# The last five items of a query convolution taken group by group, and an attention core's transposes split around values and projection

## The reference

```python
qkv = x @ w_qkv.T
q = _causal_conv1d(_causal_conv1d(q, qc1_w, qc1_b, N_HEADS), qc2_w, qc2_b, 1)   # 1024 channels, 3 taps
k = _causal_conv1d(_causal_conv1d(k, kc1_w, kc1_b, N_KV), kc2_w, kc2_b, 1)      # 256 channels
q = q.reshape(B, S, 16, 64) + 0.5 * k_mean[:, :, None, :]
k = k.reshape(B, S, 4, 64) + 0.5 * q_mean[:, :, None, :]
q, k = _rope(_l2norm(q), cos, sin), _rope(_l2norm(k) * key_temp, cos, sin)
scores = jnp.where(causal, jnp.einsum('bhqd,bhkd->bhqk', q, kg) * scale, min)
out = jnp.einsum('bhqk,bhkd->bhqd', softmax(scores), vg)
return out @ w_o.T
```

## Time and profile before

| | us |
|---|---|
| median of three runs | 2670.66 |
| the profiled execution | 2671.36 |
| its span in the trace | 2669.6 |
| query convolution, from the start of item 27 to the last matmul | 384.4 to 426.3 |
| from there to the first transpose of the attention core | 426.3 to 444.9 |
| attention core's units, first scores to last projection | 460.5 to 688.1 |

### The profile page before, as it was taken

The page is one execution under the profiler, slowest core; times in us unless marked ns, Lnnn a source line. Parts: engine busy times, 40 slices in busy tenths (PEclk is TensorE's granted clock), DMA queues, the critical chain, the costliest instruction groups (busy, mean ns, idle before and its releaser), DMA issues. The chain is left out here.

```text
span 2669.6 us, 37362 instructions
## 1 busy us (share of the span) xinstructions
PE 2489.1 (93%) x12664; PEld 1816.4 (68%) x12664; DVE 1777.2 (67%) x3189; ACT 1419.6 (53%) x2796; POOL 1490.2 (56%) x1274
## 2 busy tenths in 40 slices
PE   7999996799899789999999999999999999999967
PEld 3464443444587668878878878887787787787754
DVE  2044456577423687777777777778778778778765
ACT  2210003555222286686676676776776776776713
POOL 0043354455101248678678678677777768668642
PEclk9999998899899899999999999999999999999979
DMA  4012321000210263253352352352352352343300
GB/s 163 0 38 75 118 59 36 1 1 1 87 63 13 69 187 108 88 159 100 95 157 94 100 156 91 97 166 89 98 167 87 100 163 91 100 150 101 104 19 32
DMA packets 143628, 241.87 MB, mean 91 GB/s; under 512 B 28368, under 2 KB 48592, under 8 KB 143184
## 3 DMA queue, kind: packets, MB, share of 16 engines
q1 hardware_dynamic: 143440, 239.48, 28.7%
HBM read 232.08 MB, written 7.34 MB: 90 GB/s over the span
## 5 line engine op out<-in xcount | busy, mean ns | idle before, releaser
L1785 ACT ACTIVATE mix<-mix,sc 128x128 f32<-128x128 f32 x1024 | 310.8, 389 | 3.0 <-DMA sc<-head_scal 2.8
L2116 POOL TENSOR_TENSOR xend<-xdt,sc 128x384 f32<-128x384 f32 x128 | 106.7, 834 | 320.0 <-DVE xdt L1918 320.0
L1955 DVE SCALAR_TENSOR_TENSOR feat<-ps,chan,feat 128x511 f32<-128x511 f32 (+2 forms) x384 | 283.8, 739 | 1.8
L98 PE MATMUL ps<-xt_hi,w_in_hi 128*128 128x512 f32 x640 | 267.3, 418 | 12.8 <-ACT sg L1775 5.7
L1944 DVE TENSOR_TENSOR mix<-mix,cb 128x512 f32<-128x512 f32 x256 | 272.2, 1068 | 1.2 <-ACT mix L1791 1.2
L99 PE MATMUL ps<-xt_lo,w_in_hi 128*128 128x512 f32 x640 | 253.6, 396 | 0.0
L100 PE MATMUL ps<-xt_hi,w_in_lo 128*128 128x512 f32 x640 | 253.6, 396 | 0.0
L2132 POOL TENSOR_TENSOR w_in_lo<-w_in_raw,w_in_hi 128x512 fp32r<-128x512 f32 x158 | 211.6, 1339 | 61.1 <-ACT w_in_hi L1740 61.1
L1989 DVE TENSOR_TENSOR y_lo<-y,y_hi 128x512 fp32r<-128x512 f32 x128 | 183.0, 1430 | 81.1 <-ACT y_hi L1801 81.0
L1632 PE MATMUL ps<-w_o_hi,y_hi 128*128 128x512 f32 x512 | 207.6, 405 | 7.9 <-DVE y_lo L1989 4.3
L98 PE MATMUL ps<-xt_hi,w_g_hi 128*128 128x512 f32 x512 | 212.8, 416 | 2.2 <-DVE feat L1955 2.2
(11 more groups left out here) (288 smaller groups left out, 5943.9 us busy)
## 6 DMA issues: line engine op xcount, KB each, us to landing
mix<-row_cum SPq DMA_DIRECT2D x128, 512.0 KB, 5.7
w_in_raw<-in_w_conv_in SPq DMA_DIRECT2D x160, 256.0 KB, 3.1
w_g_raw<-in_w_gate_in SPq DMA_DIRECT2D x128, 256.0 KB, 3.5
ecb<-row_ecum SPq DMA_DIRECT2D x256, 96.0 KB, 3.4
w_o_raw<-in_w_out SPq DMA_DIRECT2D x64, 256.0 KB, 3.0
w<-in_w_c2q SPq DMA_DIRECT2D x16, 768.0 KB, 5.3
w<-in_w_c2q SPq DMA_DIRECT2D x16, 512.0 KB, 3.7
wqkv<-in_w_qkv SPq DMA_DIRECT2D x1, 3072.0 KB, 14.0
```

The costliest lines, as they stand in the source:

```text
L98: pe.matmul(out, a_hi, b_hi, start=(n == 0), stop=False)
L1785: last = act.activation(m, m, ACT.Relu, bias=sc[:, b, CUM, z, 2 * i + e:2 * i + e + 1], scale=-1.0)
L1955: dve.scalar_tensor_tensor(out=to, in0=ps[:, j % 2, 0:S - back], scalar=chan[:, bb % B, j, K1 - 1 - back:K1 - back], in1=to, op0=ALU.mult, ...
```

## The change

In the convolution `TAIL` becomes 5, with `EXTRA` = 2 items (30 and 31) that own buffers outside the rings: the space of `k1` for their token differences, of `w2k` and `head_sum` for their taps. These were last read by the key convolution, so that SP, DVE and POOL wait for `c2_ready` at `NK` there. Nothing in `schedule` moves.

```diff
-    NI, RAWK = 4 * QT, 4
+    NI, RAWK, EXTRA = 4 * QT, 4, 2
-            TAIL = WS
+            TAIL = WS + EXTRA
+            def tx_of(r, kind):
+                if last(r) < 0:
+                    return tx[:, r % WS, kind, :, :]
+                flat = k1[:, :, :, :].rearrange("p c b n -> p (c b n)")
...
+            def outer_taps(r):
+                if last(r) < 0:
+                    return w2[:, r % RAWS, 0:TAPS:2, :]
+                if last(r) == 0:
+                    return w2k[:, :, :, :].rearrange("p c t o -> p (c t o)")[:, 0:2 * BANK].rearrange("p (t o) -> p t o", t=2)
+                return head_sum[:, 0, :, :]
...
+            def freed(eng, r):
+                if last(r) >= 0:
+                    eng.wait_ge(c2_ready, NK)
+                elif r >= WS:
+                    eng.wait_ge(item_done, r - WS + 1)
...
                     for r in range(RAWS, NI):
                         p, n, c = pass_of(r)
-                        if inner_item(r - RAWS):
+                        if last(r) >= 0:
+                            sp.wait_ge(c2_ready, NK)
+                        elif inner_item(r - RAWS):
```

```diff
                         if u < NU:
                             scores(u)
+                        if 1 <= u < NU + 1:
+                            turn(u - 1, (0, 1))
                         if u % 2 == 1 and 3 <= u < NU + 3:
                             values((u - 3) // 2)
                         if u >= KV0 + LAG:
                             project(u - KV0 - LAG)
                         if 1 <= u < NU + 1:
-                            turn(u - 1)
+                            turn(u - 1, (2, 3))
...
                             for i in range(GQ):
+                                if i == GQ - 1:
+                                    copy(u - 1, 0)
...
-                        if u >= 1:
-                            for k in range(units[u - 1][1] + 1):
...
+                        for k in range(1 if u < NU else 0, ZB):
+                            copy(u - 1, k)
```

More of the change, by code:

```diff
@@ L246, in attention @@
             w1_loaded = core.sem("a_w1_loaded")
-            w2_loaded = [core.sem(f"a_w2_loaded{i}") for i in range(RAWS)]
+            w2_loaded = [core.sem(f"a_w2_loaded{i}") for i in range(RAWS + EXTRA)]
             small_loaded = core.sem("a_small_loaded")
@@ L451, in attention, with last, loaded @@
             ROPE_AT = 2 * QT + 2
-            TAIL = WS
+            TAIL = WS + EXTRA
+            def last(r):
+                return r - (NI - EXTRA)
+            def tx_of(r, kind):
+                if last(r) < 0:
+                    return tx[:, r % WS, kind, :, :]
+                flat = k1[:, :, :, :].rearrange("p c b n -> p (c b n)")
+                at = (2 * last(r) + kind) * B * PAIRS
+                return flat[:, at:at + B * PAIRS].rearrange("p (b n) -> p b n", b=B)
+            def outer_taps(r):
[4 more added lines that the diff above has]
+                return head_sum[:, 0, :, :]
+            def loaded(eng, r):
+                if last(r) < 0:
+                    eng.wait_ge(w2_loaded[r % RAWS], 16 * (r // RAWS + 1))
+                else:
+                    eng.wait_ge(w2_loaded[RAWS + last(r)], 16)
+            def freed(eng, r):
[3 more added lines that the diff above has]
+                    eng.wait_ge(item_done, r - WS + 1)
             def schedule(prepare, rope_k, evict, rope_q):
@@ L493, in _ @@
                         else:
-                            sp.dma_start(w2[:, r % RAWS, 0:TAPS:2, :], taps[:, 0:TAPS:2, :]).then_inc(w2_loaded[r % RAWS], 16)
+                            sp.dma_start(outer_taps(r), taps[:, 0:TAPS:2, :]).then_inc(
+                                w2_loaded[r % RAWS if last(r) < 0 else RAWS + last(r)], 16)
                 @blk.tensor
@@ L515, in item @@
                         if closing:
-                            pe.wait_ge(w2_loaded[r % RAWS], 16 * (r // RAWS + 1))
+                            loaded(pe, r)
                         else:
@@ L527, in item @@
                             for kind in range(2):
-                                taps = w2[:, r % RAWS, 2 * kind, :] if closing else mixed[:, r % WS, kind, :]
-                                last = pe.matmul(ps[:, 2 * j + kind, :], tx[:, r % WS, kind, b, half * P:(half + 1) * P], taps,
+                                taps = outer_taps(r)[:, kind, :] if closing else mixed[:, r % WS, kind, :]
+                                done = pe.matmul(ps[:, 2 * j + kind, :], tx_of(r, kind)[:, b, half * P:(half + 1) * P], taps,
                                                  start=(c == 0), stop=(c == QT - 1 and not closing))
                             if j == JT - 1:
-                                last.then_inc(item_done, 1)
+                                done.then_inc(item_done, 1)
                             elif c == QT - 1 and not closing:
-                                last.then_inc(pass_ready, 1)
+                                done.then_inc(pass_ready, 1)
                             if c == QT - 1 and closing:
@@ L537, in item @@
                                     tokens = head_sum[:, 1, b, half * 2 * P + e:(half + 1) * 2 * P:2]
-                                    last = pe.matmul(ps[:, 2 * j + e, :], tokens, sel[:, 0:BANK], start=False, stop=True)
-                                last.then_inc(pass_ready, 1)
+                                    done = pe.matmul(ps[:, 2 * j + e, :], tokens, sel[:, 0:BANK], start=False, stop=True)
+                                done.then_inc(pass_ready, 1)
                     for r in range(NI - TAIL):
@@ L551, in prepare @@
                         even, odd = q1[:, c, :, 0, :], q1[:, c, :, 1, :]
-                        if r >= WS:
-                            dve.wait_ge(item_done, r - WS + 1)
+                        freed(dve, r)
                         if inner_item(r):
-                            dve.tensor_tensor(tx[:, r % WS, 0, :, :], odd[:, :, 0:PAIRS], even[:, :, 1:], ALU.add).then_inc(t_one, 1)
+                            dve.tensor_tensor(tx_of(r, 0), odd[:, :, 0:PAIRS], even[:, :, 1:], ALU.add).then_inc(t_one, 1)
                             dve.wait_ge(ends_done, inner_before(r + 1))
@@ L560, in prepare @@
                         else:
-                            dve.tensor_tensor(tx[:, r % WS, 0, :, :], even[:, :, 0:PAIRS], even[:, :, 1:], ALU.subtract).then_inc(t_one, 1)
+                            dve.tensor_tensor(tx_of(r, 0), even[:, :, 0:PAIRS], even[:, :, 1:], ALU.subtract).then_inc(t_one, 1)
                     def evict(p, j):
@@ L689, in prepare @@
                             pool.tensor_tensor(ends[:, r % 2, :], w2[:, r % RAWS, 0, :], w2[:, r % RAWS, 2, :], ALU.add).then_inc(ends_done, 1)
-                        if r >= WS:
-                            pool.wait_ge(item_done, r - WS + 1)
+                        freed(pool, r)
                         if inner_item(r):
-                            pool.tensor_tensor(tx[:, r % WS, 1, :, :], even[:, :, 1:], odd[:, :, 0:PAIRS], ALU.subtract).then_inc(t_two, 1)
+                            pool.tensor_tensor(tx_of(r, 1), even[:, :, 1:], odd[:, :, 0:PAIRS], ALU.subtract).then_inc(t_two, 1)
                         else:
-                            pool.tensor_tensor(tx[:, r % WS, 1, :, :], odd[:, :, 1:], odd[:, :, 0:PAIRS], ALU.subtract).then_inc(t_two, 1)
+                            pool.tensor_tensor(tx_of(r, 1), odd[:, :, 1:], odd[:, :, 0:PAIRS], ALU.subtract).then_inc(t_two, 1)
                     def rope(u):
@@ L805, in scores, with turn @@
                                       kt[at, kv, b * S:b * S + wide], start=True, stop=True).then_inc(sc_ready, 1)
-                    def turn(u):
+                    def turn(u, tiles):
                         b, z, kv = units[u]
-                        for k in range(z + 1):
+                        for k in tiles:
+                            if k > z:
+                                continue
                             n = tiles_before[u] + k
@@ L867, in _, with copy @@
                             act.activation(dst, ps[:, n % 4, :].rearrange("p (i n) -> p i n", i=4), ACT.Copy).then_inc(turn_done, 1)
+                    def copy(u, k):
+                        if u < 0 or k > units[u][1]:
+                            return
+                        n = tiles_before[u] + k
+                        act.wait_ge(pt_ready, n + 1)
+                        if u >= 4:
+                            act.wait_ge(pv_ready, (u - 4) // 2 + 1)
+                        act.activation(prob_t[:, u % 4, k, :, :],
+                                       ps[:, 4 + n % 2, :].rearrange("p (i n) -> p i n", i=GQ), ACT.Copy).then_inc(pt_done, 1)
                     for u in range(NU + 1):
```

## The result

The changed kernel takes 2658.42 us (median of five runs, 2656.71 to 2660.05) against 2671.05 us for the kernel before, measured again beside it. The ratio is 0.9952, 95% interval 0.9937 to 0.9966. The forecast was 2660, with 0.80 for faster.

The account below looks back on a forecast made before the run. The normalising and rotating chain was taken to bound the convolution's tail, with 20.8 us of PE copy waits in the core. Tail -4.9, core -4.3 and clock -1.6 sum to -10.8 us, forecasting 2660 us, range 2650 to 2667.

Parts of the forecast that it names:

- The tail: End of the query convolution: group 0 starts two items earlier, PE becomes the limit, the block ends 4.9 us earlier.
- The core, orders and waits: Attention core: PE's split and ACT's earlier copy of tile 0, walked through 32 iterations, save 4.3 us.
- The offsets from D: Attention core, times after DVE's first mask addition: copy 0 at 3.67 us, fourth exponent at 4.2, copy 1 at 4.86.
- +0.9: Attention core, up to iteration 17: time given back after the first batch's gain of 3.9 us, leaving 2.9.
- the late exponent: Attention core: the fourth exponent comes 0.2 us later behind the early copy, delaying the last inversion where DVE limits.
- The clock: Core's first batch: shorter waits ahead of tile 2 remove one of three falls to half clock, saving 1.6 us.
- 3.9 + 1.6: Core's first batch: 3.9 us gained by the walk through the iterations, plus 1.6 us for one clock fall gone.
- A: Rival: the walk holds with no change in the clock, -9.2 us, 2661.5 us; chance 0.54 counted together with the forecast.
- C: Rival: only the tail gains, the core's gain lost as PE waits for normalised probabilities; 2665.8 us, chance 0.12.
- D: Rival: the core gains but the tail doesn't, taps or POOL's difference being late by 4 us or more; 2665, chance 0.09.
- B: Rival: the clock stays up in the core's whole first batch, 5.5 us more gain, 2654 us; chance 0.19.
- E: Rival, slower: ACT's copy 0 holds the fourth exponent for its whole 0.6 us in every unit; 2685 us, chance 0.06.

Follow-up runs that it names:

- e1: Changed kernel with the attention core's order as before, so only the convolution's tail changed: 2661.33 us, ratio 0.9965 to the kernel before.
- e3: Changed kernel with item 31's preparation moved ahead of rope_q(6) in the common order of DVE, ACT and POOL: 2656.06 us.
- e8: Changed kernel with ACT's early copy only for units of three or four key tiles, the old order for narrower ones: 2655.95 us.
- e5: Changed kernel with ACT's order as before, all copies behind the four exponents; PE's split stays: 2662.70 us.
- e6: Changed kernel with PE's order as before, the whole turn behind values and projection; ACT's early copy stays: 2675.45 us.
- e7: Changed kernel with two early copies, copy 0 ahead of the third exponent and copy 1 ahead of the fourth: 2650.55 us.
- e2: Changed kernel with EXTRA = 0, so only the attention core changed and the convolution's tail is as before: 2663.63 us.
- e4: Changed kernel with two extra matmuls in PE's wait ahead of tile 2 in iterations 1, 2, 4 and 6: 2652.42 us.

## Why the prediction was right, point by point

**The tail.** Right in all its steps. The wait for the taps moved to item 29 and cost 0.65 us (forecast 0.42), the taps of items 30 and 31 landed at 388.9 and 390.1 us, ahead of the forecast's 389.7 and 391.2, POOL's list put 1.15 us ahead of item 31 (forecast 1.5), the groups came 10.3 us apart, and the stretch lost 4.8 us (forecast 4.9). e1 shows it alone; e3 shows that POOL's list is the cause.

**The core, orders and waits.** The offsets from D were right to 0.06 us. Where the clock is out of play, in the second batch, iterations 17 to 24 gained 2.9 us (forecast 3.0), and the rest of the core gave back 1.6 (forecast 1.6). From iteration 9 to the start of 17 the forecast was +0.9; the trace has -0.2. Two things hide in that. e8 against the changed kernel shows the price of the late exponent there, +1.4 us. And the kernel before had a fall of the clock that I didn't count, at the values of iteration 13 (half clock from 552.7 to 556.1 us).

```profile
552.18 3.23 PE L827 MATMUL ps<-prob_t,v_tok 128*64 128x512 f32 x8 [0.58 <-ACT prob_t L887]
```

In the changed kernel the same eight records take 1.94 us:

```profile
541.60 1.94 PE L859 MATMUL ps<-prob_t,v_tok 128*64 128x512 f32 x8
```

With the projection behind them this was worth 2.0 us. It is absent in e5 and e8 too; e1 and e6, without PE's split, have it, but so has e7, with it. So what removes it is not shown. The forecast hadn't counted it, and without it the core would have gained 5.6 us instead of 7.6: that part is luck, and it hid the late exponent, which cost more from 9 to 17 than the +0.9 allowed for. (A reading to correct: a tile's four transposes are four records, not eight; rows with x8 are two tiles.)

**The clock.** I took one of three falls in the first batch as gone, for 1.6 us. The trace before has four stretches at half clock there, 20.5 us together; the changed kernel has three, 13.7 us. Up to iteration 9 it gained 6.2 us, the forecast was 3.9 + 1.6. That this came so close is luck as well. The four programs that issue the same instructions that far (the changed kernel, e2, e3, e8) were 6.2, 7.2, 7.0 and 2.0 us ahead of the kernel before, with 13.7, 10.3, 10.3 and 27.3 us at half clock: in e8's trace the clock fell for longer than before the change. And the ground on which I chose, that a wait of 2.2 us is nearer to 2.54 than to 1.69, doesn't hold: in e7 the clock falls behind waits of 1.2 and 1.5 us. The direction is shown by e4: fill the wait, and the clock stays. That the falls left in the changed kernel cost 4.7 us is shown too. Which of them a program gets is not explained.

**The rivals.** A (no change of the clock) lay in the forecast's own range; the clock did change. C falls: PE waited 0.8 us in all for normalised probabilities. D falls: the tail gained 4.8 us. B (the clock stays up throughout) was priced at 2654; e4, which brings it about with extra matmuls, is at 2652.4. E, the slower side, holds in one form: e6, where the copy does hold the fourth exponent. What decides is not the copy's own 0.6 us, but whether the transpose it waits for stands behind values and projection.

## What to carry to other kernels

When an engine's list holds work for two pipelines, look at what an item moved forward waits for: ACT's early copy cost 0.2 us an iteration with PE's transposes moved along, and made the core 11 us longer without. With five items in the group-by-group tail a group took 10.3 us, longer than the 9.0 of the chain that consumes it, and the next wait was in the list that prepares the last item; so a longer tail should bring nothing more (worked out, not run). Where TensorE waits in every iteration, here for 1.2 to 3.2 us, price the half clock along with the wait, and try a matmul that computes nothing in it: one of 0.86 us in each of four waits was worth 4 us of the median (2646.53 to 2642.25).

## What the runs showed of the hardware

Four programs with the same instruction order in the core's first nine iterations took 61.6, 61.8, 62.6 and 66.8 us for them, with 10.3, 10.3, 13.7 and 27.3 us at half clock, while the same program profiled twice repeated within 0.06 us. One trace of each program can't tell a difference between them that is smaller than this. A fall needs no single long wait: in e7 it came behind waits of 1.2 and 1.5 us. The exponent behind a copy starts 0.47 us after the copy did (473.64 to 474.11), though the copy alone takes 0.59.
